# A four-layer kernel on one core: batch 6's step reordered, and the last batch's first layer 2 tiles multiplied as halves

## The reference, cut to what matters

```python
x = x + (x @ W.T + (x @ lora_A[label]) @ lora_B_w.T * 0.5)             # layer 0
gi = sum(abs(x) <= thresholds)                                          # layer 1: 8 groups
d, zp = deltas[min(gi, 7)], zero_points[min(gi, 7)]
x = x + where(gi == 8, 0, (clip(round(x / d) + zp, 0, 63) - zp) * d)
x = x + x @ weight[adapter].T                                           # layer 2: 1024 x 1024
x = x + (x @ B[adapter].T) @ A[adapter].T                               # layer 3: rank 16
```

## Time and profile before

| what | value |
|---|---|
| median of three runs | 457.94 us (457.54 to 459.03) |
| the profiled execution's own time | 457.52 us |
| its span | 455.6 us |
| busy PE, DVE, ACT, POOL | 98%, 93%, 79%, 9% |
| granted TensorE clock over the span | 1.00 (2.4 GHz) |

### The profile page before, as it was taken

One profiled execution on the slowest core, in us unless ns is written; L12 is line 12 of the kernel. 1 busy time (PEld: TensorE's weight loads), 2 busy tenths in 40 slices (PEclk: granted clock), 3 DMA queues, 4 the chain that ended last, 5 costly groups with the idle time before them and its releaser, 6 DMA issues.

```text
span 455.6 us, 7843 instructions
## 1 busy us (share of the span) xinstructions
PE 445.8 (98%) x3094; PEld 407.3 (89%) x3094; DVE 422.3 (93%) x402; ACT 357.7 (79%) x331; POOL 42.8 (9%) x54
## 2 busy tenths in 40 slices
PE   8999999999999999999999999999999998999995
PEld 7899999989998999889998999889998998998784
DVE  4799989999999998999899998899969999999983
ACT  5698999998699769977799766996579858686730
POOL 3400010012200010000100010110100001000000
PEclk9999999999999999999999999999999999999999
DMA  7973462595468835785459825586353715478022
GB/s 256 343 268 105 94 173 72 138 263 164 82 199 217 255 84 158 208 241 178 82 197 219 255 81 156 147 216 166 80 197 105 173 59 147 142 224 309 1 93 92
DMA packets 35640, 75.62 MB, mean 166 GB/s; under 512 B 3988, under 2 KB 14100, under 8 KB 34836
## 3 DMA queue, kind: packets, MB, share of 16 engines
q1 hardware_dynamic: 30708, 61.50, 40.6%
q0 software_dynamic: 4896, 13.63, 17.0%
HBM read 53.10 MB, written 8.39 MB: 135 GB/s over the span
## 4 chain that ended last, share of the span: by engine, by line
PE 75%; DVE 15%; issue 6%; ACT 1%; DMA 1%; POOL 0%; DVEq 0%; SPq 0%; ACTq 0%
PE l_ps L941 35%; PE l_ps L1042 23%; PE l_ps L1054 6%; DVE quant L804 4%; DVE cand L778 4%; PE l_ps L1070 3%; PE bx_ps L997 2%; PE bx_ps L1089 2%; PE l_ps L949 1%; PE l_ps L983 1%; DVE cand L786 1%; DVE x L756 1%; DMA cand<-w 1%; DVE quant L798 1%; DVE x L855 1%
## 5 line engine op out<-in xcount | busy, mean ns | idle before, releaser
L1042 PE MATMUL l_ps<-x,w_sb 128*128 128x256 f32 x672 | 150.3, 380 | 0.9 <-DVE x L756 0.9
L804 DVE COPY_PREDICATED quant<-mask,cand 128x2048 f32<-128x2048 int8 (+2 forms) x77 | 146.0, 1896 | 0.4
L1042 PEld LDWEIGHTS l_ps<-x,w_sb 128*128 128x128 f32 x672 | 125.9, 190 | 19.4 <-issue 2.1
L589 ACT ACTIVATE cand<-x,inv_delta 128x2048 f32<-128x2048 f32 (+2 forms) x88 | 134.4, 1528 | 8.8 <-DVE quant L798 7.0
L599 ACT ACTIVATE mask<-magnitude,thr_bias 128x2048 fp8e5<-128x2048 f32 (+2 forms) x77 | 117.4, 1525 | 8.6 <-DVE quant L804 7.9
L778 DVE TENSOR_SCALAR cand<-cand,delta 128x2048 f32<-128x2048 f32 (+2 forms) x88 | 87.4, 993 | 7.9 <-ACT cand L589 7.7
L786 DVE TENSOR_SCALAR cand<-cand,lower,upper 128x2048 f32<-128x2048 f32 (+2 forms) x88 | 93.0, 1057 | 0.4
L941 PE MATMUL l_ps<-x_hi,w_hi 128*128 128x256 f32 x496 | 82.8, 289 | 0.0
L941 PE MATMUL l_ps<-x_hi,w_lo 128*128 128x256 f32 x496 | 79.7, 283 | 0.0
L941 PE MATMUL l_ps<-x_lo,w_hi 128*128 128x256 f32 x496 | 79.6, 283 | 0.0
L941 PEld LDWEIGHTS l_ps<-x_hi,w_hi 128*128 128x128 f32 x496 | 68.7, 191 | 5.0 <-issue 3.7
(11 more groups left out here) (89 smaller groups left out, 401.4 us busy)
## 6 DMA issues: line engine op xcount, KB each, us to landing
w_sb<-w SPq DMA_DIRECT2D x60, 384.0 KB, 3.7
out<-x SPq DMA_DIRECT2D x32, 256.0 KB, 2.3
x_raw<-x SPq DMA_DIRECT2D x14, 512.0 KB, 5.7
w_edge<-w SPq DMA_DIRECT2D x28, 256.0 KB, 3.8
w_lo<-w_edge POOLq DMA_DIRECT2D x28, 256.0 KB, 4.8
x_lo<-x_raw POOLq DMA_DIRECT2D x6, 1024.0 KB, 8.6
x<-a SPq DMA_DIRECT2D x7, 512.0 KB, 3.5
cand<-w SPq DMA_DIRECT2D x4, 512.0 KB, 8.0
```

Of the source, the lines that this page charges most:

```text
L589: act.activation(cand[:, c % CANDS, 0:n], x2_unit(u), ACT.Identity, bias=ROUND, scale=inv_delta[:, k:k + 1]).then_inc(rounded, 1)
L804: dve.copy_predicated(y, mask[:, m % MASKS, 0:n].bitcast(I8), t).then_inc(merged, 1)
L1042: last = nc.tensor.matmul(l2_bank(b, q)[:, i * S:(i + 1) * S], w2_block(b, o, k), x2[:, b % SLOTS, k * S:(k + 1) * S], start=(i == 0 and k ...
```

## The change

1. **Step 6 on ACT.** `drain_bx(5)`, the copy to `parts`, stands straight behind the drain of layer 0 at j = 6, ahead of the last mask; the edges' splits 1 and 2 of batch 6 come later.
2. **Step 6 on DVE.** `drain_l2(5, 0)` stands one candidate earlier (j = 0).
3. **Batch 7's edge blocks as halves.** `last_layer2(0)` becomes `last_first_part()`: first blocks 2 and 3 of all eight tiles as plain fp32 (16 products), then blocks 0 and 1 as halves (48 fp32r products). Its halves of the weights and of x2 lie in `x_hi` and `x_lo`, which layer 0 no longer needs. ACT splits the edges in units `LAST` and `LAST + 1`, POOL issues six more adding transfers, and one POOL TENSOR_TENSOR of 128x512 makes the low half of x2. SP loads the edge blocks 0 to 3 already in step 6.
4. **Layer 3 of batch 6.** Its `drain_bx` stands at j = 3 instead of 5 of unit `LAST + 2`, its `split_bx` at 5 instead of 6, and `sum_bx(6)` on PE comes after two quarters of `last_layer2(1)` instead of one.
5. `ADDED_UP = (3,)` only names what was written out before for quarter 3.

```diff
@@ SP: loads
+                    if s == B - 2:
+                        last_adapter = adapter_of(B - 1)
+                        for o in range(RING):
+                            load_last_edge(o, last_adapter)
                     load_w2(s, 1, adapter)
...
                 else:
-                    for o in range(RING):
-                        load_last_edge(o, adapter)
                     for o in range(RING, T):
@@ POOL
+            add_last_edge(RING)
+            hi, lo = x2_halves(B - 1)
+            pool.wait_ge(x2_hi_done, B)
+            pool.tensor_tensor(lo, x2[:, (B - 1) % SLOTS, 0:EX], hi.bitcast(F32), ALU.subtract)\
+                .then_inc(x2_split_done, 1)
+            for o in range(RING + 1, T):
+                add_last_edge(o)
@@ ACT
+            def split_last_edge(o):
+                act.wait_ge(last_edge_loaded[o], 16)
+                hi = last_edges(x_hi, o, 1)
+                act.activation(hi, edge_tile(B - 1, o), ACT.Copy).then_inc(w2_hi_done, 1)
+                act.wait_ge(w2_hi_done, 4 * SPLIT + 3 + o - RING)
+                act.activation(last_edges(x_lo, o, 1), hi.bitcast(F32), ACT.Copy, scale=-1.0)\
+                   .then_inc(w2_neg_done, 1)
...
                     if j == 6:
                         drain_l0(s + 1, 0)
-                        if s < SPLIT:
+                        if s < B - 2:
                             split_edges(s, 1)
-                    if j == 7:
-                        if s < SPLIT:
-                            split_edges(s, 2)
+                        else:
+                            drain_bx(s - 1)
+                    if j == 7 and s < B - 2:
+                        split_edges(s, 2)
                         drain_bx(s - 1)
                         split_bx(s - 1)
-                        if s + 1 < B - 1:
-                            drain_l0(s + 1, 1)
+                        drain_l0(s + 1, 1)
+                    elif j == 7:
+                        split_edges(s, 1)
+                        split_bx(s - 1)
+                        split_edges(s, 2)
@@ DVE
-                    if j == 1:
+                    if j == (0 if s == B - 2 else 1):
                         drain_l2(s - 1, 0)
@@ PE
+            def last_first_part():
+                b = B - 1
+                pe.wait_ge(x0_done, 2 * B)
+                pe.wait_ge(x2_done, LAST + 1)
+                for o in range(T):
+                    pe.wait_ge(last_w2_loaded[o], 16)
+                    for k in range(EDGE, PARTS[1]):
+                        nc.tensor.matmul(l2_bank(b, o // 2)[:, o % 2 * S:(o % 2 + 1) * S], w2_block(b, o, k),
+                                         x2[:, b % SLOTS, k * S:(k + 1) * S], start=(o % 2 == 0 and k == EDGE),
+                                         stop=False)
+                pe.wait_ge(x2_split_done, B)
+                x2h, x2l = x2_halves(b)
+                for o in range(T):
+                    if o >= RING:
+                        pe.wait_ge(last_edge_added[o - RING], 16)
+                    elif o % 2 == 0:
+                        pe.wait_ge(w2_added[o // 2], 16 * B)
+                    hi, lo = last_edges(x_hi, o, 1), last_edges(x_lo, o, 1)
+                    for w, v in ((hi, x2h), (hi, x2l), (lo, x2h)):
+                        for k in range(EDGE):
+                            nc.tensor.matmul(l2_bank(b, o // 2)[:, o % 2 * S:(o % 2 + 1) * S],
+                                             w[:, k * P:(k + 1) * P], v[:, k * S:(k + 1) * S],
+                                             start=False, stop=False)
...
-            last_layer2(0)
+            last_first_part()
             for q in range(4):
                 low_rank3(B - 2, q)
-            last_layer2(1, (0,))
+            last_layer2(1, (0, 1))
             sum_bx(B - 2)
-            last_layer2(1, (1, 2, 3))
+            last_layer2(1, (2, 3))
```

More of the change, by code:

```diff
@@ L48 @@
 LAST_ORDER = (0, 3, 1, 2)
+ADDED_UP = (3,)
 UNITS = ((0, 0, HW), (0, HW, HW)) + tuple((b, 0, BW) for b in range(1, B - 1))\
@@ L128, in build @@
         last_w2_loaded = [sem(f"last_w2_loaded{o}") for o in range(T)]
+        last_edge_loaded = [sem(f"last_edge_loaded{o}") for o in range(T)]
+        last_edge_added = [sem(f"last_edge_added{o}") for o in range(RING, T)]
         w2_used = sem("w2_used")
@@ L240, in split_pair, with last_edges, x2_halves @@
             return tiles[:, first:first + 2, :]
+        def last_edges(halves, first, n):
+            return halves[:, 0, first * EW:(first + n) * EW]
+        def x2_halves(b):
+            if b == B - 1:
+                return x_hi[:, b % 2, 0:EX], x_lo[:, b % 2, 0:EX]
+            return x2_hi[:, :], x2_lo[:, :]
         def a3_raw(b):
@@ L343, in store @@
                     sp.wait_ge(out_done, b * 4 + q + 1)
-                elif q == 3:
-                    sp.wait_ge(last_out_done, 1)
+                elif q in ADDED_UP:
+                    sp.wait_ge(last_out_done, ADDED_UP.index(q) + 1)
                 else:
-                    sp.wait_ge(out_done, b * 4 + q + 1)
+                    sp.wait_ge(out_done, b * 4 + [p for p in LAST_ORDER if p not in ADDED_UP].index(q) + 1)
                 sp.dma_start(out[b, q], x3[:, q * CW:(q + 1) * CW]).then_inc(out_stored[q], 16)
@@ L471, in _ @@
                     add_x(s + 2)
+                if s == SPLIT:
+                    for q in range(2):
+                        add_last_pair(q)
                 add_edges(s - 1, 3)
@@ L566, in split_edges, with split_last_pair, split_last_x2 @@
                 act.activation(split_pair(w2_hi, b, q), raw_edges(q), ACT.Copy).then_inc(w2_hi_done, 1)
-                act.wait_ge(w2_hi_done, n + 1)
+                act.wait_ge(w2_hi_done, edge_count(b, q))
                 act.activation(split_pair(w2_lo, b, q), split_pair(w2_hi, b, q).bitcast(F32), ACT.Copy, scale=-1.0)\
                    .then_inc(w2_neg_done, 1)
+            def split_last_pair(q):
+                for o in (2 * q, 2 * q + 1):
+                    act.wait_ge(last_edge_loaded[o], 16)
+                act.wait_ge(l0_done, 2 * (B - 1))
+                hi = last_edges(x_hi, 2 * q, 2)
+                act.activation(hi, x_raw[:, 2 * q * EW:2 * (q + 1) * EW], ACT.Copy).then_inc(w2_hi_done, 1)
+                act.wait_ge(w2_hi_done, 4 * SPLIT + q)
+                act.activation(last_edges(x_lo, 2 * q, 2), hi.bitcast(F32), ACT.Copy, scale=-1.0)\
+                   .then_inc(w2_neg_done, 1)
+            def split_last_edge(o):
+                act.wait_ge(last_edge_loaded[o], 16)
+                hi = last_edges(x_hi, o, 1)
+                act.activation(hi, edge_tile(B - 1, o), ACT.Copy).then_inc(w2_hi_done, 1)
+                act.wait_ge(w2_hi_done, 4 * SPLIT + 3 + o - RING)
+                act.activation(last_edges(x_lo, o, 1), hi.bitcast(F32), ACT.Copy, scale=-1.0)\
+                   .then_inc(w2_neg_done, 1)
+            def split_last_x2():
+                act.wait_ge(l0_done, 2 * B)
+                act.wait_ge(x2_done, LAST + 1)
+                act.activation(x2_halves(B - 1)[0], x2[:, (B - 1) % SLOTS, 0:EX], ACT.Copy).then_inc(x2_hi_done, 1)
             def take_magnitude(u):
@@ L656, in between @@
                         drain_l0(s, 1)
+                    if j == 4:
+                        split_last_pair(1)
                     if j == 5:
                         split_edges(s - 1, 3)
+                elif u == LAST + 1:
+                    if j in (1, 2, 3, 4):
+                        split_last_edge(RING + j - 1)
+                    if j == 1:
+                        split_last_x2()
                 elif u == LAST + 2:
+                    if j == 3:
+                        drain_bx(s - 1)
                     if j == 5:
-                        drain_bx(s - 1)
-                    if j == 6:
                         split_bx(s - 1)
@@ L704, in _ @@
             split_bx(B - 1)
-            act.wait_ge(l3_done, 4 * (B - 1) + LAST_ORDER.index(3) + 1)
-            act.activation(x3[:, 3 * CW:4 * CW], l3_bank(B - 1, 3), ACT.Copy).then_inc(last_out_done, 1)
+            for q in ADDED_UP:
+                act.wait_ge(l3_done, 4 * (B - 1) + LAST_ORDER.index(q) + 1)
+                act.activation(x3[:, q * CW:(q + 1) * CW], l3_bank(B - 1, q), ACT.Copy).then_inc(last_out_done, 1)
         @block.vector
@@ L911, in _ @@
             for q in LAST_ORDER:
-                if q != 3:
+                if q not in ADDED_UP:
                     finish(b, q)
@@ L1072, in last_layer2 @@
                                                     x2[:, b % SLOTS, k * S:(k + 1) * S],
-                                                    start=(i == 0 and k == 0), stop=(i == 1 and k == T - 1))
+                                                    start=False, stop=(i == 1 and k == T - 1))
                     if part == len(PARTS) - 2:
@@ L1102, in layer3 @@
                     pe.wait_ge(a3_split_done, b + 1)
-                on_x3 = b == B - 1 and q == 3
+                on_x3 = q in ADDED_UP
```

(9 more changed lines are left out.)

22 lines of the change are left out of this document (14 added, 8 removed).

## The result

The changed kernel took 459.68 us (median of 7 runs, 457.8 to 460.94), the kernel before 457.96 us on the same chip (7 runs, 457.13 to 459.03). The ratio is 1.0034 with a 95% interval of 1.002 to 1.0049: slower, by about 1.6 us. The forecast was 457.5 us with a range of 456.2 to 458.7 and 0.70 on "no change", so it was wrong in direction and in size. The profiled execution took 460.01 us, 2.5 us more than that of before (457.52), while the medians differ by 1.7 us: what follows adds up these two executions and not the medians.

The account below looks back on a forecast made before the run. Bound: two nearly equal chains, PE's stream and DVE's quantiser, PE later by 1.53 us at layer3_pair(6). Gain 1.47 (PE) - 0.05 (ACT) - 1.04 (POOL) = 0.38 us, so 457.94 - 0.4 = 457.5 us, range 456.2 to 458.7.

Parts of the forecast that it names:

- no change: Whole kernel: a time difference under 0.3% (1.37 us), which cannot be told from none; chance 0.70.
- The two chains: Up to layer3_pair(6): PE's stream and DVE's quantiser, PE later by 1.53 us; 1.47 us to be had.
- the 1.42 of the forecast: Whole kernel: the full gain in us if POOL's instruction holds up nothing; chance 0.15.
- Step 6: Batch 6's step: PE's waits for drain and parts go, new wait of 0.7 us at layer3_pair(5), PE 1.49 us earlier.
- The fp32r stretch: First part of batch 7's layer 2 on PE: 48 fp32r products replace half the fp32 work, taking 5.76 us.
- the stall on tile 3's load: Batch 7's layer 2: PE may wait up to 1.0 us for tile 3's main block, within its slack.
- the last adding transfer: Batch 7's layer 2, PE's last tile: a stall of at most 1.2 us on POOL's transfer, within slack.
- PE's arrival at the pair: Before layer3_pair(6): PE stands there at 435.2, 3.8 us earlier than 438.98.
- The 0.05 us for ACT: Unit LAST + 1: ACT's last two split pairs delay a candidate, holding up DVE's scaling by 0.05 us.
- the term for POOL: Unit LAST + 1: POOL's 128x512 TENSOR_TENSOR holds DVE up by 1.04 us, at most 1.8.
- rival C: PE's clock falls to 1.2 GHz in the wait before layer3_pair(6): 2 to 7 us more; chance 0.07.
- My own range for the wait: PE before layer3_pair(6): waits about 2.3 us, 3.3 with DVE 1 us later.

Follow-up runs that it names:

- x2_by_dma: Changed kernel with x2's low half made by ACT's negative and an adding transfer instead of POOL's TENSOR_TENSOR; 456.54 us, ratio 0.9959.
- no_halves: Kernel before with the new orders of step 6 and of layer 3 of batch 6, without batch 7's halves; 456.6 us, ratio 0.9971.
- pool_512: Kernel before plus one POOL TENSOR_TENSOR of 128x512, result unread, in unit LAST + 1; 459.15 us, ratio 1.0018.
- tt_first: Changed kernel with POOL's TENSOR_TENSOR ahead of the adding transfer of edge 4 instead of behind it; 458.76 us, ratio 1.0013.
- Filler: Changed kernel plus six fp32 products, result unread, in PE's wait before layer3_pair(6); 458.77 us, ratio 1.0009.
- step6_only: Kernel before with only the edits to batch 6's step (step 6); 457.99 us, ratio 1.0004.
- best_plain: no_halves with batch 6's x2 split by ACT and an adding transfer, and ACT's two layer-3 steps of batch 6 one candidate later; 456.05 us, ratio 0.9956.
- best_halves: x2_by_dma with batch 6's x2 split by ACT and an adding transfer, and ACT's two layer-3 steps one candidate later; 456.97 us, ratio 0.9975.

## Why the prediction was wrong

**Right.** The two chains and the 1.47 us to be had between them: with POOL's instruction taken out, the gain was 1.9 us (x2_by_dma), with the halves out 1.3 (no_halves), on both sides of the 1.42 of the forecast. Step 6 went as written, with its new wait (0.69 for 0.7). The fp32r stretch took 6.03 us between row starts for 5.76; the stall on tile 3's load was 0.39 of at most 1.0; no wait stood at the last adding transfer. PE's arrival at the pair was 1.2 us later than said (436.86 for 435.2, less the start's 0.43); that shortened the wait by as much and left its end where DVE had it. The 0.05 us for ACT was too small to tell.

**Wrong, the term for POOL.** "I take 1.04" was 1.80, the upper bound. With 1.80 in the sum the forecast would have been 0.4 us slower than before instead of 0.4 faster. I had scaled with columns from a narrow instruction beside a two-source one. pool_512 and tt_first show that a wide one costs 0.82 and 1.04 us if POOL is idle before it, so the size that I took was near by luck, and right for another place than the one in the code. The other 0.76 us come from the place: in the changed kernel the instruction stands directly behind a transfer issue that runs until 413.09, and DVE's instruction, begun at 412.42, did not end before POOL's TENSOR_TENSOR had. The prediction had POOL begin at DVE's next boundary, 412.91, behind the transfer, and counted POOL's instruction alone. Here DVE's instruction was held although POOL's is recorded from 412.79 only, 0.37 us after it. That DVE is held from the moment at which POOL's instruction becomes ready (412.30) would explain this and the two other traces; it was inferred, not shown apart.

**Wrong, the clock, which the sum put at nothing (rival C at 0.07).** It was no far outcome: six of the seven runs look like it. My own range for the wait, 2.3 to 3.3 us, lay wholly beyond the longest wait that the trace of before shows with a clock of 1.00, 1.47 us. I took the absence of a fall in that trace as evidence, though no wait of that length stood in it. Its mechanism and condition were right ("only if the wait really is one piece and that long"); its price, 2 to 7 us, was near: 1.7 us in the profiled run, a little under it, and in that of tt_first 2.6 with some 0.5 more under the pair, inside it. Filler shows that it is the wait: the same delay on DVE, products in the gap, clock 1.00.

The two are one chain. The 0.76 us of POOL went into the wait of 3.06, but tt_first says that 2.86 was long enough too, so the fall could have come with the 1.04 that I had taken. Of the shares, x2_by_dma and filler show that each is there; how the 1.6 us between the medians divide between them is known only roughly.

**Open.** The fall isn't in every run: of the changed kernel's 7 runs, six have a mean granted clock of 0.993 to 0.996, and one has 0.999 and took 457.8 us; of tt_first's, two with 0.999 took 457.89 and 458.19. What decides it was not found. The mean of an untraced run does not tell where its clock was low: the traced executions of no_halves, step6_only and best_plain have 0.997 from their last microseconds alone, where PE has nothing left to do, and no run of the kernel before is under 0.997. Two of the 10 runs of step6_only, its slowest (459.17 and 460.44 us), and one of the 12 of best_halves (459.22 us) show 0.996 too, so a fall inside the work may have come there now and then behind shorter waits; no trace shows one. No traced execution had a wait between 1.75 us (step6_only, clock held) and 2.86 us (fell).

## What to carry over

Before you make the waiting engine faster, ask how long its wait becomes: work taken off PE ahead of a wait for DVE is worth nothing, and in both traces with a PE wait of nearly 3 us the clock fell behind it, so either leave the work slow or fill the gap. Two reorderings that each bring nothing may bring their gain only together, when one frees PE and the other the engine that waits for PE; try them alone and together. For a GpSimd tensor instruction next to DVE's steady stream, look at what stands ahead of it in GpSimd's queue and at when it will end, not at its columns alone; and an ACT negative with an adding transfer is the cheaper way when DVE is the chain.
